# Attention scores as three fp32r products of high and low parts, in a fused transformer layer on one core

## The chip, the core and the metric

The kernel runs on one core of a Trainium2 chip. A core has five engines with a queue each: TensorE (PE, with its weight loads PEld), VectorE (DVE), ScalarE (ACT), GpSimd (POOL) and SyncE (SP), which here only issues DMA transfers. They work in their own written order and wait for one another by semaphores. The metric is the device time of one execution in microseconds.

## What is computed

128 independent batches of 32 queries with 256 features; each batch has a context of 257 rows of 192 features.

```python
x = x + xattn(layernorm(x), ctx)      # 8 heads of 64: softmax(q k^T / 8) v, then Wo and bo
x = x + attn(layernorm(x))            # gated recurrent attention over the 32 positions, 4 heads of 64
x = x + ffn(layernorm(x))             # gelu(x U1 V1 + b1) U2 V2 + b2, hidden size 1024

# in xattn, for each batch:
q = x @ Wq; k = context @ Wk; v = context @ Wv
attn = softmax(einsum('bhsd,bhld->bhsl', q, k) * scale)
out = einsum('bhsl,bhld->bhsd', attn, v) @ Wo + bo

# in attn, w, r = sigmoid(...), k, v projections of xn:
state = (1 - w_t) * state + k_t v_t^T ;  out_t = r_t state
```

## The kernel before

The batches are worked on in 16 groups of G = 8, so that a group has T = 256 tokens. The program is one long pipeline, unrolled by Python: for each i (a group) and b (0 to 7), with n = 8i+b, every engine does its share for batch n, and fills the rest with pieces of the token-wise work of neighbouring groups. This text calls such a piece of the program **step b0 to b7**. It begins on TensorE with the transposition of the probabilities of batch n.

In a step TensorE does `turn_probs(n)` (L400, four transpositions), `score(n + 1)` (L388 and L391), the fillers of `FILL1[b]`, `pv(n)` (L413 to L418), and the fillers of `FILL2[b]`. The keys are never formed: `Qk` is Wk times q, per head (tiles Qa0, Qa1, Qb, buffers `qk`), and a score is Qk times the transposed context `raw_t`. The 192 context features are a part of 128 rows (L388) and a part of 64 rows (L391), the two halves of the (query, head) rows using the two row halves of the array. All of this is in fp32. Other projections (`terms`, L331) are already written as three products of high and low parts in fp32r, a reduced format of 4 bytes: high times high, low times high, high times low.

The softmax of batch n+1 goes DVE `nmax` (L765), ACT `exps` (L624), DVE `rinv` and `probs` (L770, L772), and must be done before the next step's transposition. ACT does in each step `pt_out(n)` (L629), `exps(n + 1)`, its part of the fillers, `pc_out(n)` (L634). GpSimd waits for `probs`, takes the last context column (L962), and has a few steps of its own in `STEPS`: the decays times k and r (`hat`), residual additions, and the inverse roots of the variances.

Filler names: XT, XT2, XT3 are transpositions of the three normalised inputs; q0 to q3, z, k, r, v projections; Qa0, Qa1, Qb the three parts of Qk; Sp, Sq the products of rhat and khat (L510); O2, Y1, Y2, Y3 outputs of the three parts; Pf, H0 (with H1), H2 (with H3), Qf the feed-forward part, with H the hidden tiles whose gelu ACT computes (L691); TP and WV the value side; psp, su, i0 to i2, ti, pr, cf are VectorE's. Each filler writes one or two of four PSUM banks, taken in turn over the whole program; a bank is written again when the tile four before has been read out.

SyncE issues in each step `load_t(n + 3)` and `load_n(n + 3)` into rings of three buffers. `load_n` waits until PV of batch n has finished, and all that stands behind it waits too. In b5 the 16 small transfers of `load_tail_values` (L274) stand ahead of `load_t(n + 3)`.

## Time and profile before

| | us |
|---|---|
| median of 3 runs | 1013.85 |
| lowest, highest | 1013.67, 1015.03 |
| the profiled execution | 1017.14 |
| its span, first to last instruction | 1015.4 |
| TensorE busy | 984.8 (97%) |
| ACT, VectorE, GpSimd busy | 571.6, 497.0, 211.0 |
| one group of eight batches in the middle | 59.6 |

The profile gives for each engine its busy time, and for each group of instructions the idle time ahead of it with the instruction that ended it. The stretches of a group repeat to within some hundredths of a microsecond from group 3 to group 13, so one group is enough to read. Times inside the trace are microseconds from the span's start.

### The profile page before, as it was taken

Reading aid. Unit: us, or ns where it says so; the run is one execution under the profiler, and the core shown is the slowest. Engines: PE = TensorE matmul, PEld = TensorE weight load, DVE = VectorE, ACT = ScalarE, POOL = GpSimd, SP = SyncE. Lnnn points to the kernel's source line nnn. Section 1 sums busy time; section 2 is a strip of 40 time slices with the busy share of each in tenths; the row PEclk is TensorE's granted clock in tenths of the full one; section 3 lists DMA queues with packets and bytes.
Section 4 is the critical chain, followed back from the end, with each engine's and each line's share of the span. In section 5 each row is a group of like instructions: output and inputs, shape, how many; then the busy total and the mean of one; then the engine's idle time right before and its main releaser. Section 6 shows DMA issues by size and latency. Waiting matters only on the chain.

```text
span 1015.4 us, 21353 instructions
## 1 busy us (share of the span) xinstructions
PE 984.8 (97%) x8328; PEld 790.1 (78%) x8328; DVE 497.0 (49%) x1172; ACT 571.6 (56%) x1371; POOL 211.0 (21%) x356
## 2 busy tenths in 40 slices
PE   4999999999999999999999999999999999999997
PEld 3668787887878778787887878778787887877775
DVE  4444545463645546364554636454463545446252
ACT  3445457476574747657474765747466574746231
POOL 0010304022130302213031221303122040302130
PEclk9999999999999999999999999999999999999799
DMA  8232222222222221222222122222213222212000
GB/s 299 90 91 84 86 84 68 90 61 67 84 78 88 74 78 55 85 85 77 77 85 77 54 87 85 77 76 86 68 55 92 86 69 77 75 60 64 1 12 21
DMA packets 58002, 78.90 MB, mean 78 GB/s; under 512 B 10288, under 2 KB 39856, under 8 KB 57904
## 3 DMA queue, kind: packets, MB, share of 16 engines
q1 hardware_dynamic: 56192, 76.38, 24.3%
q8 instruction: 68, 1.11, 0.4%
q10 hardware_dynamic: 1712, 1.16, 0.4%
q14 instruction: 30, 0.25, 0.1%
HBM read 73.05 MB, written 4.46 MB: 76 GB/s over the span
## 4 chain that ended last, share of the span: by engine, by line
PE 69%; DVE 15%; ACT 12%; issue 2%; POOL 1%; DMA 0%; POOLq 0%; DVEq 0%
PE gb L331 13%; PE scores L388 9%; PE scores L391 6%; PE gb L450 6%; PE gb L510 5%; PE acc L417 5%; PE ptp L400 5%; PE acc L413 4%; DVE inv L865 4%; ACT probs L624 3%; PE acc L418 3%; PE gb L559 3%; DVE probs L772 2%; DVE nmax L765 2%; ACT hid L691 2%
## 5 line engine op out<-in xcount | busy, mean ns | idle before, releaser
L624 ACT ACTIVATE probs<-scores,nmax 128x257 f32<-128x257 f32 x256 | 119.4, 472 | 176.3 <-DVE nmax L765 176.1
L765 DVE TENSOR_REDUCE nmax<-scores 128x2 f32<-128x514 f32 x128 | 88.6, 692 | 215.8 <-PE scores L391 215.8
L962 POOL TENSOR_TENSOR ptm<-probs,head 128x32 f32<-128x32 f32 x128 | 33.1, 258 | 550.0 <-DVE probs L772 550.0
L388 PE MATMUL scores<-raw_t,qk 128*128 128x257 f32 x512 | 133.2, 383 | 1.3 <-ACT qk L664 1.3
L388 PEld LDWEIGHTS scores<-raw_t,qk 128*128 128x128 f32 x512 | 87.8, 191 | 8.8 <-issue 1.7
L772 DVE TENSOR_TENSOR probs<-probs,rinv 128x514 f32<-128x514 f32 x128 | 89.4, 699 | 4.4
L391 PE MATMUL scores<-raw_t,qk 64*128 64x257 f32 x512 | 90.7, 431 | 0.0
L417 PE MATMUL acc<-pt,raw_n 128*128 128x256 f32 x256 | 90.0, 433 | 0.0
L400 PE MATMUL ptp<-ident,probs 128*128 128x128 f32 x512 | 78.6, 276 | 9.2 <-DVE probs L772 7.5
L413 PEld LDWEIGHTS acc<-pt,raw_n 128*64 128x64 f32 x1024 | 55.8, 137 | 38.2 <-issue 24.5
L413 PE MATMUL acc<-pt,raw_n 128*64 128x128 f32 x1024 | 83.3, 284 | 0.6 <-ACT pt L629 0.4
L629 ACT ACTIVATE pt<-ptp 128x512 f32<-128x512 f32 x128 | 77.1, 602 | 11.8 <-PE ptp L400 9.9
L418 PE MATMUL acc<-pt,raw_n 128*128 128x256 f32 x256 | 76.6, 381 | 0.0
L770 DVE RECIPROCAL rinv<-rsum 128x2 f32<-128x2 f32 x128 | 21.0, 164 | 111.2 <-ACT probs L624 110.5
L634 ACT ACTIVATE pc<-acc 128x384 f32<-128x384 f32 x128 | 63.8, 498 | 20.2 <-PE acc L418 20.1
L1035 POOL TENSOR_TENSOR rstd<-ve,half 128x2 f32<-128x2 f32 x48 | 33.4, 696 | 200.4 <-DVE ve L753 200.3
L400 PEld LDWEIGHTS ptp<-ident,probs 128*128 128x128 f32 x512 | 60.3, 143 | 17.4 <-DVE probs L772 14.4
L391 PEld LDWEIGHTS scores<-raw_t,qk 64*128 64x128 f32 x512 | 38.7, 185 | 43.0 <-issue 43.0
L510 PEld LDWEIGHTS gb<-rhat,khat 64*128 64x128 f32 x1024 | 64.2, 193 | 3.2 <-issue 2.0
L510 PE MATMUL gb<-rhat,khat 64*128 64x32 f32 x1024 | 62.2, 273 | 1.3 <-POOL khat L1002 1.2
L331 PE MATMUL gb<-wo_h,o_h 128*128 128x256 f32 x192 | 57.1, 297 | 0.1
L417 PEld LDWEIGHTS acc<-pt,raw_n 128*128 128x128 f32 x256 | 38.3, 188 | 22.1 <-issue 22.1
(145 smaller groups left out, 2311.1 us busy)
## 6 DMA issues: line engine op xcount, KB each, us to landing
raw_t<-in_ctx_t SPq DMA_DIRECT2D x128, 258.0 KB, 2.9
raw_n<-in_ctx_n SPq DMA_DIRECT2D x128, 192.0 KB, 2.4
xb<-in_x SPq DMA_DIRECT2D x16, 256.0 KB, 2.7
vsp<-tail_values SPq DMA_DIRECT2D x256, 2.0 KB
out<-ob SPq DMA_DIRECT2D x16, 256.0 KB, 2.2
xin<-in_x SPq DMA_DIRECT2D x15, 256.0 KB, 2.9
khat<-in_wq ACTq DMA_DIRECT2D x1, 512.0 KB, 4.4
wv<-in_wv SPq DMA_DIRECT2D x1, 512.0 KB, 6.3
```

Of the source, the lines that this page charges most:

```text
L331: last = mm(out_, w, x, start=k == 0, stop=k == len(products) - 1)
L388: mm(scores[:, r, 0:L], w[:, b, r * P:(r + 1) * P], x[:, 0, 0:L], start=True, stop=False)
L391: mm(scores[:, r, 0:L], w[half, b, 2 * P:3 * P], x[half, 1, 0:L], start=False, stop=True).then_inc(s["scores_ready"], 1)
L400: last = nc.tensor.transpose(ptp[:, t, r * P:(r + 1) * P], probs[n % 2][:, r, t * P:(t + 1) * P], ident[:])
L413: last = mm(acc[64 * k:64 * k + 64, 1, 0:P], x[:, t, P:C], pt[:, t, k * P:(k + 1) * P], start=t == 0, stop=t == 1)
L417: mm(acc[:, 0], x[:, 0, 0:P], pt[:, 0], start=True, stop=False)
L418: mm(acc[:, 0], x[:, 1, 0:P], pt[:, 1], start=False, stop=True).then_inc(s["acc_ready"], 1)
L510: last = mm(out_[:, 0, t_].rearrange("p (b i) -> p b i", i=S)[:, :, block], khat[r0:r0 + 64, keys:keys + P], rhat[r0:r0 + 64, c * T + t * ...
L624: go(probs[n % 2][:, r, 0:L], scores[:, r, 0:L], ACT.Exp, bias=nmax[:, r:r + 1], accum_out=rsum[:, r:r + 1]).then_inc(s["exp_ready"], 1)
L629: go(pt[:], ptp[:], ACT.Copy).then_inc(s["ptev_ready"], 1)
L765: v_.tensor_reduce(nmax[:], scores[:, :, 0:L], AX.X, ALU.max, negate=True)\
L772: v_.tensor_tensor(p_[:, :, 0:L], p_[:, :, 0:L], rinv[:].rearrange("p (r o) -> p r o", o=1).to_broadcast([P, 2, L]), ALU.mult).then_inc(s[ ...
```

## The change

- **Scores.** `score` makes three fp32r products for each fp32 product: Qk high times context high, Qk low times context high, Qk high times context low. It reads 258 columns (LP) instead of 257.
- **Context parts.** `t_h` (the context rounded to fp32r) and `t_l` (what is left) have two buffers each. For batch m both are made in step m-2: the high part by ACT (`high`, between `pt_out` and `exps`), for two batches in eight by GpSimd; the low part by GpSimd (`parts`, ahead of all else in its step). TensorE waits for `low_ready`, and so does `load_t`, in place of the scores.
- **Qk parts.** ACT writes `qk_h`, VectorE subtracts for `qk_l` (items Qa0+1, Qa1+1, Qb+1 of `GAPS`).
- **Gelus.** H0 and H2 stand in the same step b7. Other fillers move: see the two tables `FILL1` and `FILL2`.
- **rhat** moves from GpSimd (r0, r1) to VectorE (`rh`), with the sigmoid's halving folded into Wo2, and the khat items move to b5.
- **Buffers.** Several tiles share memory (qs in hid, kt in ob, vt in at, qf in pr, xt3 in xt2, xn2 in xn1, xt1 in o), with waits for their last readers. The start-up constants go from before the first batch to step b3 of group 0; the third and later loads of `xin` go from b7 to b0 of the next step of i.

```diff
-FILL1 = [["Sq", "Qf", "WV"], ["O2"], [], ["Qa0"], [], ["Qa1", "H0"], ["Qb"], ["Sp", "H2"]]
-FILL2 = [[], ["Y3", "Y1", "XT"], ["q0", "q2", "Y2", "XT2"], ["z", "q1", "XT3"], ["q3", "r", "Pf"], ["k"], ["v"],
+FILL1 = [["Sq", "Qf", "WV"], ["O2"], [], ["Qa0"], ["Qa1"], ["Qb"], [], ["Sp", "H0", "H2"]]
+FILL2 = [[], ["Y3", "Y1", "XT"], ["Y2", "XT2", "q0", "q2"], ["z", "q1", "q3", "XT3"], ["k"], ["r"], ["Pf", "v"],
          ["TP"]]
...
+POOL_HIGH = (3, 4)
+def by_pool(m):
+    return (m - 2) % G in POOL_HIGH
...
             def load_t(n):
                 if n >= RING:
-                    sp.wait_ge(s["scores_ready"], 2 * (n - RING + 1))
+                    sp.wait_ge(s["low_ready"], n - RING + 1)
                 sp.dma_start(raw_t[n % RING][:], ctxt_v[n]).then_inc(ctxt_in[n % RING], 16)
...
             def score(n):
                 g, b = n // G, n % G
-                pe.wait_ge(ctxt_in[n % RING], 16 * (n // RING + 1))
+                pe.wait_ge(s["low_ready"], n + 1)
...
+                terms_ = ((w_h, h), (w_l, h), (w_h, l))
                 for r in range(2):
-                    mm(scores[:, r, 0:L], w[:, b, r * P:(r + 1) * P], x[:, 0, 0:L], start=True, stop=False)
-                for r in range(2):
-                    half = slice(64 * r, 64 * r + 64)
-                    mm(scores[:, r, 0:L], w[half, b, 2 * P:3 * P], x[half, 1, 0:L], start=False,
-                       stop=True).then_inc(s["scores_ready"], 1)
+                    for k, (w, x) in enumerate(terms_):
+                        mm(scores[:, r, 0:LP], w[:, b, r * P:(r + 1) * P], x[:, 0], start=k == 0, stop=False)
+                for k, (w, x) in enumerate(terms_):
+                    for r in range(2):
+                        half = slice(64 * r, 64 * r + 64)
+                        last = mm(scores[:, r, 0:LP], w[half, b, 2 * P:3 * P], x[half, 1], start=False, stop=k == 2)
+                        if k == 2:
+                            last.then_inc(s["scores_ready"], 1)
...
+            def high(m):
+                act.wait_ge(ctxt_in[m % RING], 16 * (m // RING + 1))
+                if m > 1:
+                    act.wait_ge(s["scores_ready"], 2 * (m - 1))
+                go(t_h[m % 2][:], raw_t[m % RING][:], ACT.Copy).then_inc(s["high_act_ready"], 1)
...
                     if 0 <= n < B:
                         pt_out(n)
+                    if (i, b) == (FIRST, 4):
+                        high(0)
+                    if 0 < n + 2 < B and not by_pool(n + 2):
+                        high(n + 2)
                     if 0 <= n + 1 < B:
                         exps(n + 1)
...
+            def parts(m):
+                if m > 1:
+                    pool.wait_ge(s["scores_ready"], 2 * (m - 1))
+                if by_pool(m):
+                    pool.wait_ge(ctxt_in[m % RING], 16 * (m // RING + 1))
+                    p_.tensor_copy(t_h[m % 2][:], raw_t[m % RING][:]).then_inc(s["high_pool_ready"], 1)
+                    pool.wait_ge(s["high_pool_ready"], m + 1 - act_highs(m))
+                else:
+                    pool.wait_ge(s["high_act_ready"], act_highs(m))
+                p_.tensor_tensor(t_l[m % 2][:], raw_t[m % RING][:], t_h[m % 2][:].bitcast(F32), ALU.subtract)\
+                    .then_inc(s["low_ready"], 1)
...
-                    [["Y2-2"], ["XT2-1", "xn2-2"], []],
-                    [[], ["su-1"], ["i0-1", "i1-1", "i2-1", "ti-1"]],
-                    [["r-1", "ln0+2"], ["pr-1", "cf-1"], []],
-                    [["xn0+2"], [], []],
-                    [[], [], ["S0-1", "S1-1"]]]
+                    [["Y2-2"], ["XT2-1", "xn2-2"], ["Qa0+1"]],
+                    [[], ["su-1"], ["Qa1+1", "ti-1", "i0-1"]],
+                    [[], ["cf-1"], ["Qb+1", "i1-1"]],
+                    [["i2-1", "pr-1"], [], ["rh-1", "ln0+2"]],
+                    [[], ["S0-1", "S1-1"], ["xn0+2"]]]
```

The order of instructions shows where the pieces stand. First ACT in steps b6 and b7, before. `pt` begins a step, `probs` are the exponentials, `qk` the copies of Qb, `hid` the gelus of H2.

```order
L629 ACTIVATE pt<-ptp 128x512
L624 ACT_TABLE_LOAD
L624 ACTIVATE probs,rsum<-scores,nmax 128x257 x2
L664 ACTIVATE qk<-gb 128x2x8x32 x2
L634 ACTIVATE pc<-acc 128x12x32
L682 ACTIVATE vt<-gb 128x512
L629 ACTIVATE pt<-ptp 128x512
L624 ACTIVATE probs,rsum<-scores,nmax 128x257 x2
L691 ACT_TABLE_LOAD
L691 ACTIVATE hid<-gb,vecs 128x256 x4
L634 ACTIVATE pc<-acc 128x12x32
```

The same two steps of the changed kernel; the lines are those of its own text, `t_h` is the high copy, the `at` row is the copy of v.

```order
L659 ACTIVATE pt<-ptp 128x512
L655 ACTIVATE t_h<-raw_t 128x516
L648 ACTIVATE probs,small<-scores,small 128x257 x2
L664 ACTIVATE pc<-acc 128x12x32
L720 ACTIVATE pf<-gb 128x256
L716 ACTIVATE at<-gb 128x512
L659 ACTIVATE pt<-ptp 128x512
L655 ACTIVATE t_h<-raw_t 128x516
L648 ACTIVATE probs,small<-scores,small 128x257 x2
L725 ACT_TABLE_LOAD
L725 ACTIVATE hid<-gb,vecs 128x256 x8
L664 ACTIVATE pc<-acc 128x12x32
```

In b6 and b7 a copy of raw_t for the batch after next now stands ahead of the exponentials, the copies of Qb are gone to b5, and all eight gelus stand in b7.

SyncE from b4 to b7 of the changed kernel, where the order is the same as before but for the load of `xin`, which stood ahead of the third raw_t load:

```order
L270 DMA raw_n<-in_ctx_n 128x384
L293 DMA vsp<-tail_values 8x64 x16
L265 DMA raw_t<-in_ctx_t 128x516
L270 DMA raw_n<-in_ctx_n 128x384
L265 DMA raw_t<-in_ctx_t 128x516
L270 DMA raw_n<-in_ctx_n 128x384
L265 DMA raw_t<-in_ctx_t 128x516
L270 DMA raw_n<-in_ctx_n 128x384
L275 DMA xin<-in_x 128x2x256
```

The first raw_t behind the vsp transfers is that of batch 8g+8, the first batch of the next group. Only what waits for it has moved.

## Rows read from the trace of the kernel before

**Rows 1.** The page: busy time, share of the span, instructions.

```profile
PE 984.8 (97%) x8328; PEld 790.1 (78%) x8328; DVE 497.0 (49%) x1172; ACT 571.6 (56%) x1371; POOL 211.0 (21%) x356
```

**Rows 2.** Stretches b0 to b7 of group 9: length, engines' busy time, clock, DMA.

```profile
535.15:545.97 10.82, 10.82 (x123) 7.87 (x122) 3.54 (x8) 4.96 (x11) 0.24 (x1) 1.00 0.15 44
545.97:554.56 8.59, 8.59 (x74) 7.49 (x73) 3.53 (x7) 3.04 (x8) 0.24 (x1) 1.00 0.38 110
554.56:561.42 6.86, 6.86 (x54) 5.87 (x53) 4.72 (x13) 3.04 (x9) 0.94 (x2) 1.00 0.44 144
561.42:568.43 7.01, 7.01 (x56) 5.93 (x55) 4.34 (x12) 5.42 (x14) 0.93 (x2) 1.00 0.19 57
568.43:574.95 6.52, 6.52 (x48) 5.38 (x47) 4.20 (x9) 4.20 (x11) 1.27 (x2) 1.00 0.15 43
574.95:581.69 6.74, 6.74 (x53) 5.53 (x52) 5.98 (x19) 4.11 (x9) 2.02 (x4) 1.00 0.03 6
581.69:588.10 6.41, 6.26 (x54) 4.48 (x52) 1.56 (x3) 6.37 (x16) 4.17 (x7) 1.00 0.43 131
588.10:594.76 6.66, 6.66 (x68) 5.58 (x69) 2.25 (x5) 5.02 (x12) 3.35 (x6) 1.00 0.30 94
sum 59.61, PE 59.46 PEld 48.13 DVE 30.11 ACT 36.15 POOL 13.18; mean PE 7.43 PEld 6.02 DVE 3.76 ACT 4.52 POOL 1.65
```

**Rows 3.** Timeline of ACT and VectorE in b1: start, duration, instruction, idle before.

```profile
548.88 0.48 ACT L624 ACTIVATE probs<-scores,nmax 128x257 f32<-128x257 f32 x1 [1.67 <-DVE nmax L765]
...
548.15 0.69 DVE L765 TENSOR_REDUCE nmax<-scores 128x2 f32<-128x514 f32 x1 [1.67 <-PE scores L391]
...
550.13 0.69 DVE L772 TENSOR_TENSOR probs<-probs,rinv 128x514 f32<-128x514 f32 x1
```

**Rows 4.** Timeline of TensorE in b1: the score, and two fp32r products.

```profile
546.40 1.03 PE L388 MATMUL scores<-raw_t,qk 128*128 128x257 f32 x4
547.37 0.70 PE L391 MATMUL scores<-raw_t,qk 64*128 64x257 f32 x4
...
551.53 0.28 PE L331 MATMUL gb<-wo_l,o_h 128*128 128x256 f32 x1
551.65 0.28 PE L331 MATMUL gb<-wo_h,o_h 128*128 128x256 f32 x1
```

**Rows 5.** Timeline of TensorE in b4 and b5: PV, half-row pairs, next step.

```profile
568.43 0.60 PE L400 MATMUL ptp<-ident,probs 128*128 128x128 f32 x4
...
570.47 0.66 PE L413 MATMUL acc<-pt,raw_n 128*64 128x128 f32 x8
...
576.89 0.38 PE L363 MATMUL gb<-qs,wk 64*128 64x256 f32 x1
...
577.76 0.38 PE L549 MATMUL gb<-pf,v 64*128 64x256 f32 x1
...
578.72 0.66 PE L413 MATMUL acc<-pt,raw_n 128*64 128x128 f32 x8
...
581.69 0.27 PE L400 MATMUL ptp<-ident,probs 128*128 128x128 f32 x1
```

**Rows 6.** Groups by line: busy time, mean ns, idle before.

```profile
L652 ACT ACTIVATE xt_h<-xt 128x512 fp32r<-128x512 f32 x16 | 10.1, 629 | 0.5
L691 ACT ACT_TABLE_LOAD x28 | 35.9, 1283 | 0.5
L1025 POOL TENSOR_TENSOR xb<-xb,bo 128x512 f32<-128x512 f32 x16 | 20.5, 1279 | 0.0
L818 DVE TENSOR_TENSOR o_l<-gb,o_h 128x512 fp32r<-128x512 f32 x32 | 20.7, 687 | 64.1 <-ACT o_h L666 64.0
```

**Rows 7.** Line L772 (minimum, median, maximum ns), and GpSimd's groups at L1002.

```profile
L772 DVE TENSOR_TENSOR probs<-probs,rinv x128: 694/695/1121, 24.6 to 940.1; 128x514 f32<-128x514 f32 x128
...
L1002 POOL TENSOR_TENSOR khat<-ke,cf 128x128 f32<-128x128 f32 x16 | 12.8, 800 | 2.9 <-DVE cf L878 0.7
L1002 POOL TENSOR_TENSOR khat<-ke,cf 128x256 f32<-128x256 f32 x16 | 10.4, 651 | 0.0
```

**Rows 8.** SyncE's timeline b4 to b6; landing of raw_t; waits of its reader.

```profile
572.59 9.36 SPq L274 DMA_DIRECT2D vsp<-tail_values  x16
582.00 0.44 SPq L246 DMA_DIRECT2D raw_t<-in_ctx_t  x1
...
DMA to landing us min/median/max: 2.6/2.9/9.6
...
  DMA raw_t<-in_ctx_t: 0.2, 1
```

**Rows 9.** Idle times of TensorE, and the granted clock (column after the busy times) behind them.

```profile
25.35 0.73 PE L400 MATMUL ptp<-ident,probs 128*128 128x128 f32 x4 [2.81 <-DVE probs L772]
...
25.80:29.20 3.40, 3.40 (x14) 1.91 (x14) 0.17 (x1) 0.60 (x1) 0.00 (x0) 0.50 0.00 0
...
942.63 0.64 PE L510 MATMUL gb<-rhat,khat 64*128 64x32 f32 x8 [1.16 <-POOL khat L1002]
...
954.20:957.60 3.40, 3.40 (x26) 1.73 (x28) 0.78 (x2) 0.00 (x0) 0.00 (x0) 0.50 0.00 0
...
984.69 0.65 PE L559 MATMUL gb<-hid,u 128*64 128x256 f32 x4 [1.28 <-ACT hid L691]
...
984.70:990.00 5.30, 5.13 (x74) 4.45 (x74) 0.77 (x2) 0.39 (x1) 3.20 (x4) 1.00 0.01 3
```

More of the change, by code:

```diff
@@ L102, with act_highs @@
 BANK = bank_table()
-HATS = 9
+HATS = 7
+POOL_HIGH = (3, 4)
+def by_pool(m):
+    return (m - 2) % G in POOL_HIGH
+def act_highs(m):
+    return sum(not by_pool(j) for j in range(m + 1))
 DECAYS = 5
@@ L158, in build @@
         pt = sb("pt", [P, LT, 256])
-        nmax, rsum, rinv = sb("nmax", [P, 2]), sb("rsum", [P, 2]), sb("rinv", [P, 2])
-        qk = [sb(f"qk{i}", [P, G, 256 + P]) for i in range(2)]
+        small = sb("small", [P, 8])
+        nmax, rsum, rinv, warm = (small[:, 2 * k:2 * k + 2] for k in range(4))
+        qk_h, qk_l = ([sb(f"{n}{i}", [P, G, 256 + P], F32R) for i in range(2)] for n in ("qk_h", "qk_l"))
+        t_h, t_l = ([sb(f"{n}{i}", [P, 2, LP], F32R) for i in range(2)] for n in ("t_h", "t_l"))
         pc = sb("pc", [P, H + H // 2, T])
@@ L190, in build @@
         s2 = sb("s2", [P, 8, P])
[L193 to L206 removed]
+        o2_h, o2_l, xt3, xn2 = xt2_h, xt2_l, xt2, xn1
+        pf = sb("pf", [P, T])
+        wxt_raw, ww_raw, vt_all = hid[:, 0:2], hid[:, 2:4], rhat[:]
+        tail_t = ke[:, 0:256].rearrange("p (c b) -> p c b", c=2)
+        mask_raw, bw_raw = ke[:, 256:256 + P], ke[:, 384:386]
+        wq_raw, kv2_raw = khat[:, 0:1024], khat[:, 1024:2048]
+        wr2_raw, wo2_raw = (x[:].rearrange("p c d -> p (c d)") for x in (at, xt2))
+        wo_raw = s2[:].rearrange("p t q -> p (t q)")
         scores = ps("scores", [P, 2, 512])
@@ L301, in _ @@
                         load_tail_values(i)
-                    if b == 7 and i + 3 < NG:
-                        load_x(i + 3)
+                    if b == 0 and 3 <= i + 2 < NG:
+                        load_x(i + 2)
                     if n + RING < B:
@@ L643, in step @@
                     if n == "XT":
[L644 removed]
+                        go(xt1_h, t[:], ACT.Copy).then_inc(s["xt1_h_ready"], 1)
                     elif n == "XT2":
```

115 lines of the change are left out of this document (65 added, 50 removed).

## Prediction

> **What bounds the kernel now.** I read the page's busy times first, then the stretches of one group of eight batches, then the matmuls in order of time, and last the queue of SyncE. TensorE is busy for 97% of the span [rows 1]. The group from 535.15 us is cut at the first transposition of each batch into eight stretches, which I call steps b0 to b7 (step b of group g transposes the probabilities of batch n = 8g+b, computes the scores of n+1, and fills in other work). They add to 59.61 us; TensorE is idle for 0.15 us of that, all in b6, where ACT is busy for 6.37 of 6.41 us [rows 2]. So matmul time is the bound nearly everywhere, and what TensorE saves counts in full as long as nothing new is late at the start of a step. What must be in time there is the softmax of n+1: score, maximum, exponentials, reciprocal, normalisation. From the exponentials' start (548.88) to the end of the normalisation (550.13 + 0.69) it takes 1.94 us, and from the maximum's start 2.67 [rows 3]. With 0.07 us after the scores and 0.05 before the next transposition a step can't be shorter than about 2.10 + 2.8 = 4.9 us before, and 4.7 after; all eight have room.
>
> **Scores.** An fp32 product is two instructions in the trace. Four for 128 rows go from 546.40 to 547.37, then those for 64 rows follow [rows 4]. Eight fp32 instructions of 64 rows and 256 columns, two at a time, fill 577.76 - 576.89 = 0.87 us: one holds the array 0.217 us [rows 5]; four fill 0.87 of the 0.97, and 0.10 go to the switch to 64 rows, which stays. An fp32r product of 256 columns is one instruction and follows the last after 0.118 us (551.53, 551.65) [rows 4]. Six of these for four fp32: 0.71 for 0.87, saves 0.16. The 64-row products run two at a time on different row halves: 0.217 us for a pair in fp32. For a pair in fp32r no row exists. Bounds: 0.118 if they run together like the fp32 ones, 0.236 if one after the other. I take 0.118, since the fp32 pairs, the nearest row, do run together [rows 5]. Three pairs for two: 0.35 for 0.43, saves 0.08. Together 0.24 us a batch; at the other bound it is a loss of 0.11. 128 batches: 30 us, if all of it shows.
>
> **What ACT and GpSimd get.** The high copy is an ACT copy of 128x516 from SBUF; the nearest is 128x512 with 0.629 us. The gelus go from two table switches a group to one: two loads of 1.28 us less (one to gelu, one back), against six copies of 0.63; so ACT gains 1.2 us a group on 36.15, no bound [rows 2, 6]. The low part on GpSimd is a subtraction of two SBUF tiles of 516 columns: 1.28 us by its 128x512 addition [rows 6]; the high copies of two batches a group lie between 0.6 and 1.28. Some 12.8 us more on its 13.2, of 60: it has room, and a low part begins some 1.9 us into its step and is needed 0.44 us into the next. VectorE gets six Qk subtractions of 0.69 [rows 6]; they stand behind the normalisation, push the next maximum by up to 0.7 us in b5 and b6, and are covered by 0.5 to 1 us of room there. The eight gelus run from about 5.3 to 8.2 us after b7's start and end 0.9 us into b0, the longest step: covered. Before the second pair of hidden tiles TensorE waits some 0.1 us for two banks. Shared buffers and their waits (qf in pr, kt in ob, vt in at, xt3 in xt2) have sources that are done a step earlier: nothing.
>
> The trace has one place where VectorE and GpSimd get in each other's way: the normalisation takes 0.695 as a rule and 1.121 once, and GpSimd's 128x128 product takes 0.80 where the 128x256 one takes 0.65 [rows 7]. The Trainium skill says why ("SBUF — State Buffer", section "Who interferes with whom"): a VectorE instruction with two SBUF inputs and a GpSimd instruction that reads SBUF exclude each other for their whole length. By that rule each of the 128 new subtractions could hold a normalisation up by 1.28 us; the order places them 1 to 2 us ahead of it, so the sum would be the same but for a tenth of a microsecond in b6.
>
> **The fillers** move only between steps. Y2 and XT2 stand ahead of q0 and q2; q3 goes from b4 to b3 (+0.71 there); b4 loses q3, r and Pf and gains Qa1 and k; b5 has Qb and r; b6 has Pf and v; b7 gains H0 (0.87). With -0.24 each: b0 10.58, b1 8.35, b2 6.62, b3 7.48, b7 7.38 (with the wait for banks). b4 has its PV at 2.04 - 0.24 + 0.87 = 2.67 us, then PV and k take 2.97 as in b5 of before (578.72 to 581.69): 5.64. In the same way b5 5.83 and b6 5.78: 17.25 us for b4 to b6. Unhindered, a group would take 57.7.
>
> **The wait that I expect.** Before, raw_t(m) is first read by TensorE in step m-1. Now ACT copies it in step m-2, ahead of the exponentials of m-1, and ACT works in order. For seven batches of eight the load lands early enough. For m = 8g+8 it doesn't: SyncE issues it behind raw_n(8g+7), which waits for PV of 8g+4 (b4), and behind the 16 small transfers of vsp, 9.36 us long. Before, it is issued at 582.00, 13.57 us after b4's start, with PV at 2.04 [rows 5, 8]. Now PV stands 0.63 later: 14.20. It lands 2.9 us later (2.6 the least) [rows 8], at 17.1. ACT would copy it 1.3 us into b6, that is at 12.8. It waits 4.3 us, and the exponentials of 8g+7 wait behind it. Then copy 0.65 with start, 1.94 to the end of the normalisation, 0.05: b7 starts at 14.20 + 2.9 + 0.05 + 0.65 + 1.94 + 0.05 = 19.8 instead of 17.25. TensorE has done all it may and stands idle for 2.5 us. The group is then 10.58 + 8.35 + 6.62 + 7.48 + 19.8 + 7.38 = 60.2, 0.6 more than before.
>
> The rest: groups 2 to 14 (13) 0.6 each, 8 us. Group 15 has no load behind its vsp transfers: -1.9. Group 1, with fewer fillers, about +1. Group 0: b4 to b6 again 19.8 in place of 15.9 and the other five steps -1.2: +2.7; constants now stand in VectorE's b3, but their delay (some 4 us) is swallowed by this same wait. The Qk low part ahead of the first score: one subtraction, +0.7. The last 64 us: no term that I can see. Sum: 8 - 1.9 + 1 + 2.7 + 0.7 = +10.5 us on the profiled run's 1017.14, or, by the same difference, 1013.85 + 10.5 = 1024 in the median.
>
> **The clock.** In this trace the granted clock fell from 2.4 to 1.2 GHz after an idle time of 2.81 us (at 25.8, for 3.4 us) and after 1.16 us followed by the narrow products of rhat and khat (from 944 on, and still at 957.6, though TensorE was busy throughout), and stayed at 2.4 GHz after 1.28 us [rows 9]. An idle time of 2.5 us is nearer to the first, and b7 begins with a transposition and a score and then has these narrow products. 3.4 us at half clock lose 1.7, 13.6 us some 6; I take 3.5 a fall. Whether all 15 waits bring one can't be read from three cases: I take half, 26 us; the ends are 0 and 15 x 4 = 60.
>
> **Rivals.**
> - *The forecast*: wait and falls in part of the groups: 1024 + 26 = about 1049 us; with 5 to 15 falls 1035 to 1084. Chance 0.62.
> - *Wait without falls*, as after the idle 1.28 us: 1024, between 1016 (landing 2.6, a smaller start) and 1034. Chance 0.22.
> - *The load comes in time* (the other side). The wait decides nothing if raw_t(8g+8) lands by 17.25 - 2.69 = 14.56 us after b4's start, 2.5 us earlier than computed: if the vsp transfers took under 7 us or PV of b4 ended earlier. For it: before, TensorE waits for such a load once, for 0.2 us [rows 8]. Against it: 9.36 us is the issue time of SyncE itself, the same in every group, and 2.6 the least landing. Then each of 16 groups saves 1.9, the start costs some 1.5: 1013.85 - 29 = 985. Chance 0.08.
> - *Half-row pairs don't run together*: +0.35 a batch in the five steps outside b4 to b6, 28 us on top of the first or second case: 1050 to 1080. Chance 0.05, and the remaining 0.03 for anything later still, a second late softmax among it.
>
> **Numbers.** Predicted 1049 us. The range goes from 1016 (no falls, landing at its least) to 1085 (a fall in each group) and leaves out the full gain and a little above. A difference of 0.2% (2 us) is what a measurement can tell from no change: faster 0.09, within it 0.03 (the wait costing just what the scores save), slower 0.88.
>
> **What would show it.** ACT's copy t_h in b6 idle about 4 us before it with the transfer of raw_t named, once a group and in no other step; TensorE idle some 2.5 us before the transposition of 8g+7; b4 to b6 19.8 us together; score 1.26 us from its first to the next product instead of 1.50; two table loads a group; half clock in stretches after that idle time. I am wrong if the copy in b6 waits for nothing, if the clock row stays at full, or if a 64-row pair takes 0.24 us.

## The result, and the profile after

The changed kernel takes 1059.8 us in the median of 4 runs (1055.1 to 1068.8), where the kernel before took 1014.4 beside it (1013.7 to 1016.9): 1.046 times as long, 95% interval 1.042 to 1.050. The forecast was 1049 with a range of 1016 to 1085. The runs of the changed kernel differ by 13.7 us among themselves, those of before by 3.2. The profiled execution is the longest of the four, 1068.8 us with a span of 1066.6.

First the page of the changed kernel: busy time of the engines as in [rows 1], then the granted clock in 40 slices, and two groups of new instructions (the ACT copy t_h and GpSimd's t_l).

```profile
PE 989.1 (93%) x8840; PEld 832.3 (78%) x8840; DVE 613.2 (57%) x1285; ACT 581.3 (54%) x1439; POOL 367.8 (34%) x484
...
PEclk9889889999999999999998999999899999999998
...
L1032 POOL TENSOR_TENSOR t_l<-raw_t,t_h 128x516 fp32r<-128x516 f32 x128 | 164.6, 1286 | 263.8 <-PE scores L413 161.5
...
L655 ACT ACTIVATE t_h<-raw_t 128x516 fp32r<-128x516 f32 x96 | 61.3, 639 | 67.0 <-DMA raw_t<-in_ctx_t 67.0
```

TensorE went from 97% to 93% of the span: it now waits, and some of its busy time is at half clock. The last row names the wait: ACT's copy of the context stood 67.0 us idle for the load of raw_t. In the table of waits (total us, times, longest) it is 15 waits, one a group:

```profile
ACT t_h L655 <- DMA raw_t<-in_ctx_t: 67.0, 15, 5.7
```

Then one group, group 6, cut at the transpositions into b0 to b7 as in [rows 2] (length, busy time of PE, PEld, DVE, ACT, POOL, clock, DMA share, GB/s):

```profile
380.92:391.91 10.99, 10.82 (x126) 7.94 (x126) 3.68 (x8) 5.73 (x13) 1.53 (x2) 1.00 0.22 67
391.91:400.25 8.34, 8.34 (x77) 7.69 (x76) 3.28 (x7) 3.56 (x9) 1.52 (x2) 1.00 0.35 113
400.25:407.19 6.94, 6.84 (x58) 6.08 (x56) 5.43 (x13) 3.61 (x10) 1.95 (x2) 1.00 0.44 142
407.19:414.79 7.60, 7.59 (x64) 6.80 (x65) 5.93 (x14) 6.01 (x16) 4.88 (x7) 1.00 0.19 63
414.79:420.45 5.66, 5.66 (x50) 4.87 (x49) 3.58 (x9) 3.73 (x11) 0.64 (x2) 1.00 0.05 6
420.45:426.26 5.81, 5.81 (x58) 4.75 (x57) 5.52 (x11) 4.01 (x10) 3.79 (x5) 1.00 0.12 36
426.26:434.41 8.15, 5.79 (x46) 4.94 (x44) 5.36 (x9) 3.75 (x10) 4.61 (x7) 1.00 0.45 147
434.41:441.94 7.53, 7.52 (x80) 6.40 (x81) 4.61 (x14) 5.91 (x15) 3.99 (x5) 1.00 0.01 2
sum 61.02, PE 58.38 PEld 49.47 DVE 37.40 ACT 36.31 POOL 22.91; mean PE 7.30 PEld 6.18 DVE 4.68 ACT 4.54 POOL 2.86
```

TensorE does 58.4 us of work where it did 59.5, and the group is 61.0 long instead of 59.6. The idle time stands in b6 (2.36 us), with 0.17 in b0 and 0.10 in b2. The chain through b6, from the timelines of SyncE, ACT, VectorE and TensorE (start, duration, instruction, idle before and what ended it):

```profile
419.58 9.36 SPq L293 DMA_DIRECT2D vsp<-tail_values  x16
428.98 0.44 SPq L265 DMA_DIRECT2D raw_t<-in_ctx_t  x1
```

```profile
431.74 0.63 ACT L655 ACTIVATE t_h<-raw_t 128x516 fp32r<-128x516 f32 x1 [4.19 <-DMA raw_t<-in_ctx_t]
432.29 0.46 ACT L648 ACTIVATE probs<-scores,small 128x257 f32<-128x257 f32 x1
...
433.52 0.84 DVE L811 TENSOR_TENSOR probs<-probs,small 128x514 f32<-128x514 f32 x1
...
434.42 0.66 PE L423 MATMUL ptp<-ident,probs 128*128 128x128 f32 x4 [2.36 <-DVE probs L811]
```

The load is issued 14.19 us after b4's start (forecast 14.20), the copy begins at 16.95 (17.15), b7 at 19.63 (19.8).

In groups 1 to 14 TensorE's idle time in front of b7 lies between 2.31 and 4.60 us, and what varies is the load: SyncE takes 9.36 us over the 16 transfers in nine of these groups and up to 10.64 in the others (in group 8 one of the sixteen takes 1.60 us instead of 0.54), and raw_t lands 2.68 to 3.02 us after its issue, in group 11 after 4.29.

Last the clock. Group 8 had a wait in b6 like every other (3.36 us, one of the longer ones), and what followed ran at 1.2 GHz (column after the busy times: 0.50):

```profile
559.08 0.66 PE L423 MATMUL ptp<-ident,probs 128*128 128x128 f32 x4 [3.36 <-DVE probs L811]
```

```profile
560.20:570.40 10.20, 10.20 (x68) 8.24 (x67) 3.48 (x11) 6.13 (x15) 3.62 (x4) 0.50 0.01 2
```

That b7 took 12.11 us instead of 7.53. In this execution the clock fell behind 7 of the 15 waits, for 3.4 to 13.7 us. Idle times of 2.31 to 2.53 us were followed by no fall in seven groups and by one in the eighth; 3.06 us by none; the other six, 2.64 to 4.60 us, by one each.

### The profile page after: what moved, and what is told of

Its sections match the earlier page's. It is cut to its first block, busy times and chain, and to the rows that moved or that the text cites. A ratio compares the mean times of both kernels' runs of the same rounds, so it can differ in the third digit from the quotient of the medians.

```text
span 1066.6 us, 23095 instructions
## 1 busy us (share of the span) xinstructions
PE 989.1 (93%) x8840; PEld 832.3 (78%) x8840; DVE 613.2 (57%) x1285; ACT 581.3 (54%) x1439; POOL 367.8 (34%) x484
## 4 chain that ended last, share of the span: by engine, by line
PE 61%; SPq 13%; DVE 8%; ACT 6%; issue 6%; DMA 5%; POOL 2%; DVEq 0%; POOLq 0%; ACTq 0%
SPq L293 13%; PE gb L350 9%; PE scores L409 6%; PE gb L473 6%; PE gb L534 5%; PE acc L440 5%; PE scores L413 5%; PE ptp L423 4%; PE acc L436 4%; DMA raw_t<-in_ctx_t 4%; PE acc L441 3%; ACT probs L648 3%; PE gb L573 3%; PE gb L583 3%; DVE xn L798 3%
## 5 line engine op out<-in xcount | busy, mean ns | idle before, releaser
L1032 POOL TENSOR_TENSOR t_l<-raw_t,t_h 128x516 fp32r<-128x516 f32 x128 | 164.6, 1286 | 263.8 <-PE scores L413 161.5
L648 ACT ACTIVATE probs<-scores,small 128x257 f32<-128x257 f32 x256 | 119.1, 471 | 143.2 <-DVE small L804 143.0
L804 DVE TENSOR_REDUCE small<-scores 128x2 f32<-128x514 f32 x128 | 88.2, 689 | 122.5 <-PE scores L413 122.4
L655 ACT ACTIVATE t_h<-raw_t 128x516 fp32r<-128x516 f32 x96 | 61.3, 639 | 67.0 <-DMA raw_t<-in_ctx_t 67.0
L811 DVE TENSOR_TENSOR probs<-probs,small 128x514 f32<-128x514 f32 x128 | 90.9, 710 | 4.4
L409 PE MATMUL scores<-t_h,qk_h 128*128 128x258 f32 x256 | 85.6, 335 | 2.2 <-DVE qk_l L858 2.2
L809 DVE RECIPROCAL small<-small 128x2 f32<-128x2 f32 x128 | 20.7, 162 | 112.4 <-ACT probs L648 112.4
L436 PEld LDWEIGHTS acc<-pt,raw_n 128*64 128x64 f32 x1024 | 57.2, 140 | 30.2 <-issue 22.3
L409 PE MATMUL scores<-t_h,qk_l 128*128 128x258 f32 x256 | 74.6, 291 | 0.0
L409 PE MATMUL scores<-t_l,qk_h 128*128 128x258 f32 x256 | 74.4, 291 | 0.0
L858 DVE TENSOR_TENSOR qk_l<-gb,qk_h 128x512 fp32r<-128x512 f32 x96 | 61.6, 683 | 8.2 <-ACT qk_h L695 8.2
```

The source lines that it names most:

```text
L409: mm(scores[:, r, 0:LP], w[:, b, r * P:(r + 1) * P], x[:, 0], start=k == 0, stop=False)
L436: last = mm(acc[64 * k:64 * k + 64, 1, 0:P], x[:, t, P:C], pt[:, t, k * P:(k + 1) * P], start=t == 0, stop=t == 1)
L648: go(probs[n % 2][:, r, 0:L], scores[:, r, 0:L], ACT.Exp, bias=nmax[:, r:r + 1], accum_out=rsum[:, r:r + 1]).then_inc(s["exp_ready"], 1)
L804: v_.tensor_reduce(nmax[:], scores[:, :, 0:L], AX.X, ALU.max, negate=True)\
L811: v_.tensor_tensor(p_[:, :, 0:L], p_[:, :, 0:L], rinv[:].rearrange("p (r o) -> p r o", o=1).to_broadcast([P, 2, L]), ALU.mult).then_inc(s[ ...
L1032: p_.tensor_tensor(t_l[m % 2][:], raw_t[m % RING][:], t_h[m % 2][:].bitcast(F32), ALU.subtract)\
```

## The experiments

Each kernel was measured beside the kernel before on the same chip; a difference between two changed kernels is that of their medians and can cross chips, where the kernel before gave 1014.1 to 1015.5 us. "The group" is the middle of groups 3 to 13.

### The late load taken away

> The changed kernel with the 16 vsp transfers moved on SyncE from b5 to b7, between the loads raw_t and raw_n of that step; all else as in the changed kernel. Theory (raw_t of 8g+8 stands behind the vsp transfers and ACT's copy in b6 waits for it): ACT no longer waits for that transfer, b6 falls from 8.3 to about 5.8 us, TensorE's idle time of 2.5 us before the first transposition of b7 is gone, the clock falls behind it are gone too; 15 x 2.6 = 39 us and some 16 to 20 us of half clock: 1060 - 57 = about 1003 us (998 to 1010). Rival (it is the copies and subtractions themselves, on ACT and GpSimd, that make the softmax late): less than 10 us change, 1050 or more.

```diff
-                    if b == 5 and i < NG:
-                        load_tail_values(i)
...
                     if n + RING < B:
                         load_t(n + RING)
+                    if b == 7 and i < NG:
+                        load_tail_values(i)
+                    if n + RING < B:
                         load_n(n + RING)
```

Measured: 1018.0 us (1017.7 to 1019.3), 1.0043 (1.0027 to 1.006). The wait of t_h is gone from the table, b4 to b6 takes 17.84 us instead of 19.8, the clock stays at full from 84 to 988 us. So the load behind the 16 transfers is the cause of most of the loss. But 1018 is not the 1003 that was expected: the group is 59.23, not 57.7, and step b0 of group 1 takes 11.71 us where the kernel with the transfers in b6 (below) has 7.19. There WV of group 0 (L474) waits for the values that now land too late:

```profile
  DMA vsp<-tail_values: 2.9, 1
```

> Control: the kernel before with the same move of the vsp transfers from b5 to b7. Theory: nothing there reads raw_t before the step that needs it, so 1014 +- 2 us. Rival (the place of the vsp transfers costs by itself, by the DMA engines or SyncE's order): a change of more than 2 us, and part of what the move brings in the changed kernel would be no part of this explanation.

The same edit, made on the kernel before. Measured: 1020.3 (1020.0 to 1021.6), 1.0066 (1.005 to 1.0083): a miss, by 6 us. The middle groups are unchanged (59.5 to 59.6); b0 of group 1 went from 7.41 to 13.12, and b0 of group 2 from 9.09 to 9.88, with a wait of 0.71 us for the same transfers. It is the place of the transfers in b7 that costs, in groups 1 and 2 alone.

### The same, with the transfers in b6

The edit is the one above with `b == 6`.

> The changed kernel with one edit: the 16 transfers of vsp are issued in b6, between raw_t and raw_n, instead of in b5; nothing else. Theory: with them in b7 (measured 1018.02 us) the steady group was 59.23 us and group 1 alone paid some 4.5 us, because WV of group 0 waited for transfers that landed late. In b6 they stand one step earlier, so that this 4.5 us goes and nothing else changes: 1018.0 - 4.5 = 1013.5 us (1011 to 1016), steady group 59.2, b4 to b6 17.8 us, b0 of group 1 about 8 us in place of 11.71, no fall of the clock behind b6. Rival: the transfers stand in front of loads in b6 as they did in b5, and b4 to b6 is 19.8 us again in some groups with a fall of the clock behind it: above 1030 us. The kernel with four moves (992.92) minus this one is then what the three moves on ACT and VectorE are worth: 20.6 us by theory, 1.2 us in each of 13 groups and some 5 us in the others.

> The kernel before with the same edit: the transfers of vsp in b6, between raw_t and raw_n. With them in b7 it was 1020.31 us, 6 above the kernel before, all of it in groups 1 and 2. If that was the late landing in front of WV of group 0, one step earlier takes it away: 1014.4 (1012 to 1017), steady group 59.6 as in the kernel before, since there no engine waited for the load behind them. If the move itself costs something on any queue, it stays at 1018 or above; if the load behind the transfers did cost something in the kernel before, it falls under 1012.

Measured: the changed kernel with it 1013.7 us (1011.5 to 1017.1, 12 runs), 0.9989 (0.9976 to 1.0002); the kernel before with it 1015.8 (1013.1 to 1017.3), 1.0007 (0.9994 to 1.0019). Both as the theory had it. In the kernel before the place of the transfers is worth nothing; in the changed kernel it is worth 46 us (47, if each is held against the kernel before beside it). The change without its late load is no faster and no slower than the kernel before. Here are b6 and the group's sum of the first of the two, and TensorE's first instruction of b7:

```profile
581.98:588.35 6.37, 5.79 (x47) 4.94 (x45) 5.21 (x9) 3.61 (x10) 4.75 (x7) 1.00 0.24 73
...
sum 59.29, PE 58.40 PEld 49.52 DVE 37.25 ACT 36.27 POOL 23.07; mean PE 7.30 PEld 6.19 DVE 4.66 ACT 4.53 POOL 2.88
```

```profile
588.35 0.66 PE L424 MATMUL ptp<-ident,probs 128*128 128x128 f32 x4 [0.58 <-DVE probs L812]
```

An idle time of 0.58 us is left in b6, for the normalisation, and no load is late.

### The idle time filled, for the clock alone

> The changed kernel with five more fp32 products (ident x v1, 256 columns, into the ptp bank that is free then) at the end of TensorE's b6, in groups 0 to 14: they fill about 2.2 us of the idle time and compute nothing that is used. Theory (the rest of the loss is the half clock that follows the idle time): b4 to b6 stay at 19.7 us, no fall of the clock behind b6, b7 7.5 us in every group: 1060 - 16 (the excess of b7 over 7.5 us, summed over the groups) - a few = about 1040 us (1036 to 1045), and the spread between executions shrinks. Rival (the clock costs nothing that the late load doesn't cost anyway): 1055 to 1062.

```diff
                     for name, g in behind:
                         steps[name](g)
+                    if b == 6 and 0 <= i < NG - 1:
+                        for k in range(5):
+                            mm(ptp[:, 0], ident[:], v1[:, 0:256], start=True, stop=True)
```

Measured: 1043.1 us (1041.9 to 1044.2), 1.0292 (1.0272 to 1.0312). The wait is there as before (b6 and b7 of group 8 and, below, the stretch of nearly all groups, clock in the third column from the right):

```profile
540.04:548.13 8.09, 7.96 (x56) 6.69 (x54) 5.33 (x9) 3.74 (x10) 4.57 (x7) 1.00 0.46 141
548.13:555.66 7.53, 7.52 (x80) 6.39 (x81) 4.61 (x14) 5.92 (x15) 4.00 (x5) 1.00 0.03 12
```

```profile
64.80:1040.00 975.20, 950.84 (x8684) 801.78 (x8682) 576.57 (x1218) 550.99 (x1369) 350.66 (x461) 1.00 0.23 71
```

b7 is 7.52 us in every group from 2 on. So the clock's share of the loss is 1059.8 - 1043.1 = 16.7 us, and it is also the scatter: the runs now lie within 2.2 us instead of 13.7. The wait itself is the rest of the 46: 1043.1 - 1013.7 = 29.4 us.

### The copy behind the exponentials, in b6 only

> The changed kernel with ACT's high copy behind the exponentials in b6 alone. Theory (the exponentials of 8g+7 are late because they stand behind the copy): the softmax of 8g+7 is in time, b6 is 5.8 us; now the score of 8g+8 in b7 waits for the low part: landing 17.1 + copy 0.7 + subtraction 1.3 = 19.1 us after b4's start, where the score is due at 17.25 + 0.44 = 17.7: idle 1.4 us in b7 in place of 2.5 before it. 15 x 1.1 = 16 us less and fewer falls of the clock: about 1033 us (1024 to 1045). Rival (the exponentials are late for the transfer's other effects): no change, 1055 or more.

```diff
-                    if 0 < n + 2 < B and not by_pool(n + 2):
+                    if 0 < n + 2 < B and not by_pool(n + 2) and b != 6:
                         high(n + 2)
                     if 0 <= n + 1 < B:
                         exps(n + 1)
+                    if 0 < n + 2 < B and b == 6:
+                        high(n + 2)
```

Measured: 1054.7 (1050.8 to 1056.2), 1.0397 (1.0371 to 1.0424), far over what was expected. The order of ACT was indeed what held b7 up: b4 to b6 is 17.84. But the score in b7 now waits for the low part, as expected:

```profile
483.43 0.66 PE L423 MATMUL ptp<-ident,probs 128*128 128x128 f32 x4 [0.57 <-DVE probs L813]
485.75 0.39 PE L409 MATMUL scores<-t_h,qk_h 128*128 128x258 f32 x1 [1.67 <-POOL t_l L1034]
```

Two idle times, 0.57 and 1.67 us, with a transposition between them, and this b7 took 14.02 us, part of it at half clock. The clock fell behind b6 in 5 of the 15 groups; where it held, b7 took 8.6 in the middle, 1.1 more than with no wait. The first half of the theory stands (who blocks whom); the second half, that shorter idle times leave the clock alone, fell.

### Two of the sixteen transfers behind the load

> The changed kernel with 14 of the 16 vsp transfers in b5 as there, and two moved to b7 between raw_t and raw_n. Theory (b7 starts at the issue of raw_t of 8g+8 plus 5.5 us): raw_t is issued 2 x 0.586 = 1.2 us earlier, b4 to b6 19.7 - 1.2 = 18.5 us, TensorE idle 1.2 to 1.4 us behind b6 in groups 2 to 14. Without clock falls 1043 (the kernel with a filled idle time) - 15 x 1.2 = 1025 us; whether an idle time of 1.3 us brings falls is what this run tells: none, 1023 to 1027; some, up to 1040. Rival (the late load is a matter of the DMA engines' backlog, not of the queue's order): b4 to b6 stay above 19.

```diff
                     if b == 5 and i < NG:
-                        load_tail_values(i)
+                        load_tail_values(i, range(7))
...
                     if n + RING < B:
                         load_t(n + RING)
+                    if b == 7 and i < NG:
+                        load_tail_values(i, range(7, 8))
```

Measured: 1039.4 (1036.2 to 1049.8), 1.0265 (1.0207 to 1.0323). `load_tail_values` gets the heads as an argument; 14 transfers stay ahead of the load and 2 go behind it. The load is earlier by the 1.17 us of two transfers, and b4 to b6 is 18.44 to 18.55 us in seven groups, as expected: the wait scales with SyncE's queue, by the time of the transfers that were moved. Here a b7 with no fall of the clock, and one with:

```profile
619.02 0.66 PE L426 MATMUL ptp<-ident,probs 128*128 128x128 f32 x4 [1.20 <-DVE probs L814]
```

```profile
619.02:626.55 7.53, 7.53 (x80) 6.41 (x81) 4.61 (x14) 5.89 (x14) 3.99 (x5) 1.00 0.02 6
```

```profile
494.84 0.33 PE L426 MATMUL ptp<-ident,probs 128*128 128x128 f32 x1 [2.70 <-DVE probs L814]
```

```profile
494.84:506.93 12.09, 12.09 (x81) 10.15 (x81) 4.61 (x14) 6.75 (x17) 3.99 (x5) 0.58 0.00 1
```

In this profile idle times of 1.17 to 1.27 us in b6 were followed by no fall, seven times in seven, and 1.56 us by none; the other seven, 1.89 to 4.26 us, were followed by one each. Within this profile the clock goes with the length of the idle time, but 2.31 to 2.53 us brought a fall only once in eight in the changed kernel above. The idle time differs from group to group by the load again: in the seven short cases raw_t is issued 13.02 to 13.10 us after b4's start and lands in 2.72 to 2.79 us; in the others it is issued at 13.23 to 13.73, or lands only after 3.60 to 4.71, or both.

### The two copies ahead of the normalisation, in b0

> The changed kernel with the vsp transfers in b7 (as in e1_vsp_later) and with VectorE's copies of S2 and S3 in b0 ahead of the normalisation instead of behind it. Theory (in b0 the exponentials are late by the table load behind the eight gelus, the copies of S2 and S3 behind the normalisation with them, and the WV products wait for S2's bank): b0 10.98 falls to about 10.65 us; 13 x 0.33 = 4 us less than 1018, 1014 (1012.5 to 1015.5). Rival (the 0.4 us in b0 are the products' own time): 1018 and b0 10.98.

```diff
-            GAPS = [[["psp-1"], [], ["S2-2", "S3-2", "WV0-1", "WV1-1"]],
+            GAPS = [[["psp-1"], ["S2-2", "S3-2"], ["WV0-1", "WV1-1"]],
```

Added to the first experiment's kernel. Measured: 1014.9 (1011.9 to 1017.2, 10 runs), 1.0001 (0.9984 to 1.0018), against 1018.0 without; b0 is 10.59 instead of 10.98. What held WV up was a bank that VectorE read out behind a normalisation. Why the normalisation is late is read from ACT's timeline in b0, and no run tests it. In the changed kernel, group 6 (b0 from 380.92):

```profile
382.18 0.70 ACT L655 ACTIVATE t_h<-raw_t 128x516 fp32r<-128x516 f32 x1
382.89 1.28 ACT L648 ACT_TABLE_LOAD   x1
384.19 0.48 ACT L648 ACTIVATE probs<-scores,small 128x257 f32<-128x257 f32 x1
```

The eight gelus are over 0.56 us into b0, and `pt` starts only 0.11 us later than before (0.78 instead of 0.67). The table load starts 0.68 us later (1.97 instead of 1.29), most of it for the high copy that now stands ahead of it, and the exponentials start at 3.27 instead of 2.94.

### Four moves together

> The changed kernel with the vsp transfers in b6 between raw_t and raw_n, S2 and S3 copies ahead of the normalisation in b0, VectorE's maximum ahead of xn1 in b2 and ahead of i2 and pr in b6. Theory (with the late load gone, what is left is VectorE being late in b2 and b6, and S2's bank in b0): b0 10.65, b2 6.65, b6 5.85 us, no idle time of TensorE over 0.2 us from group 2 to 14; a group of 58.1 in place of 59.2: 14 x 1.1 = 15 us, and 4 us in group 1, whose b0 waited for the vsp transfers: 1018 - 19 = about 999 us (995 to 1004), faster than the kernel before. Rival (the late maximum in b6 comes from TensorE or ACT): b6 stays at 6.36 and the time above 1008.

```diff
-                    if b == 5 and i < NG:
-                        load_tail_values(i)
...
+                    if b == 6 and i < NG:
+                        load_tail_values(i)
...
-            GAPS = [[["psp-1"], [], ["S2-2", "S3-2", "WV0-1", "WV1-1"]],
+            GAPS = [[["psp-1"], ["S2-2", "S3-2"], ["WV0-1", "WV1-1"]],
...
-                    [["XT+1", "xn1-1"], [], []],
+                    [["XT+1"], ["xn1-1"], []],
...
-                    [["i2-1", "pr-1"], [], ["rh-1", "ln0+2"]],
+                    [[], ["i2-1", "pr-1"], ["rh-1", "ln0+2"]],
```

Measured: **992.9 us** (992.0 to 994.6), 0.9779 (0.9761 to 0.9797), under the expected 995 to 1004 and 2.2% faster than the kernel before. Against the kernel with only the transfers moved it is 20.8 us less; so three moves of VectorE's items, none of which removes an instruction, are worth nearly as much as the faster scores (23.9 us, below). The page, b2, b6 and the sum of group 9:

```profile
PE 955.5 (97%) x8840; PEld 809.0 (82%) x8840; DVE 611.8 (62%) x1285; ACT 584.8 (59%) x1439; POOL 368.1 (37%) x484
```

```profile
546.92:553.60 6.68, 6.68 (x58) 6.13 (x57) 6.47 (x17) 4.22 (x11) 3.37 (x5) 1.00 0.50 150
...
572.61:578.46 5.85, 5.79 (x46) 4.93 (x44) 5.63 (x9) 3.42 (x10) 4.57 (x7) 1.00 0.23 75
...
sum 58.00, PE 57.94 PEld 49.44 DVE 37.33 ACT 36.63 POOL 22.85; mean PE 7.24 PEld 6.18 DVE 4.67 ACT 4.58 POOL 2.86
```

TensorE's idle time is down to 0.06 us a group.

### The score's share

> e10_four_moves with the scores as one fp32 product again (Qk high times context high, read as fp32; the low parts are still made and not used). Theory (the three fp32r products save 0.24 us a batch where nothing else is late): 128 x 0.23 = 29 us slower than e10_four_moves. Rival (half-row pairs in fp32r or the reads of the low parts cost it again): less than 15 us slower.

```diff
-                terms_ = ((w_h, h), (w_l, h), (w_h, l))
+                h, w_h = h.bitcast(F32), w_h.bitcast(F32)
+                terms_ = ((w_h, h),)
...
-                        last = mm(scores[:, r, 0:LP], w[half, b, 2 * P:3 * P], x[half, 1], start=False, stop=k == 2)
-                        if k == 2:
+                        last = mm(scores[:, r, 0:LP], w[half, b, 2 * P:3 * P], x[half, 1], start=False, stop=True)
+                        if k == 0:
```

The kernel is that of the four moves. Measured: 1016.8 us (1015.7 to 1019.7, 10 runs), 23.9 more than with the three products, where 29 were expected. That is 0.19 us a batch. In b3 the step went from 7.53 to 7.76, in b6 only from 5.83 to 5.89, in part because VectorE holds its end up in the faster kernel (b6 is 5.72 there in the groups where TensorE doesn't wait for it). The score of b3 in the changed kernel, with fp32r, and the same place in the kernel of this experiment, with fp32 (TensorE's timelines):

```profile
407.61 0.37 PE L409 MATMUL scores<-t_h,qk_h 128*128 128x258 f32 x1
407.82 0.28 PE L409 MATMUL scores<-t_h,qk_l 128*128 128x258 f32 x1
407.94 0.28 PE L409 MATMUL scores<-t_l,qk_h 128*128 128x258 f32 x1
...
408.51 0.39 PE L413 MATMUL scores<-t_h,qk_h 64*128 64x258 f32 x2
...
408.97 0.37 PE L382 MATMUL gb<-hid,wk 64*128 64x256 f32 x1
```

```profile
568.41 1.04 PE L411 MATMUL scores<-t_h,qk_h 128*128 128x258 f32 x4
569.38 0.71 PE L415 MATMUL scores<-t_h,qk_h 64*128 64x258 f32 x4
569.91 0.38 PE L383 MATMUL gb<-hid,wk 64*128 64x256 f32 x1
```

From its first product to the next filler the score takes 1.36 us instead of 1.50 (forecast 1.26). Six fp32r products for 128 rows take 0.90 us to the first of the 64-row ones, not 0.81 (six at 0.118 and 0.10 for the switch): the first of them holds the array for 0.21. Four fp32 instructions take 0.97. The score is thus 0.14 us shorter, and there is a second part: from the start of the step to the first product of the score it is 0.35 to 0.41 us instead of 0.43 to 0.47. The two together make up most of the 0.18 to 0.25 us by which every step but b6 differs.

### GpSimd's subtraction taken away

> The changed kernel with the vsp transfers in b7 (as in e1_vsp_later) and GpSimd's subtraction of the low part replaced by a memset of t_l to zero, which reads nothing from SBUF and is shorter (the low part of the context is left out). Theory (VectorE and GpSimd exclude each other, and that makes VectorE late in b2 and b6): in b2 the second xn takes 0.4 instead of 1.3 us, in b5 the first cf copy 0.2 instead of 0.73; the cf steps beside the khat items stay long; b2 6.6 us, b6 6.0 us: 13 x 0.7 = 9 us less than 1018, about 1009 (1006 to 1012). Rival (the VectorE work of Qk itself makes it late): durations and time as in e1_vsp_later.

```diff
-                p_.tensor_tensor(t_l[m % 2][:], raw_t[m % RING][:], t_h[m % 2][:].bitcast(F32), ALU.subtract)\
-                    .then_inc(s["low_ready"], 1)
+                p_.memset(t_l[m % 2][:].bitcast(F32), 0.0).then_inc(s["low_ready"], 1)
```

Measured: 1003.3 us (1002.1 to 1004.7), 14.7 less than the first experiment's kernel, where 9 were expected. b2 went from 6.94 to 6.64 to 6.68 and b6 from 6.36 to between 5.85 and 6.03. VectorE's and GpSimd's timelines in b2, first of the changed kernel, then without the subtraction:

```profile
402.94 1.62 DVE L798 TENSOR_SCALAR xn<-x,mv,rstd 128x256 f32<-128x256 f32 x2 [0.28 <-POOL rstd L1105]
404.48 0.68 DVE L804 TENSOR_REDUCE small<-scores 128x2 f32<-128x514 f32 x1
...
402.80 1.28 POOL L1032 TENSOR_TENSOR t_l<-raw_t,t_h 128x516 fp32r<-128x516 f32 x1
```

```profile
558.99 0.83 DVE L799 TENSOR_SCALAR xn<-x,mv,rstd 128x256 f32<-128x256 f32 x2 [0.28 <-POOL rstd L1105]
559.74 0.68 DVE L805 TENSOR_REDUCE small<-scores 128x2 f32<-128x514 f32 x1
...
558.83 0.53 POOL L1033 MEMSET t_l<- 128x516 f32 x1
```

The same two VectorE instructions take 1.62 us beside the subtraction (the first of them 1.29) and 0.83 beside the memset, and the maximum behind them starts that much later. The two steps give 8.6 us in the groups 3 to 14 (0.72 each); groups 1, 2 and 15 give 3 more (2.98 by their lengths), and the last 3 are the clock: the first experiment's profile has 6.8 us at half clock from 988.7 on, this one has none there. By the two steps alone the expected 9 was right.

### The loops over the row halves exchanged

> e10_four_moves with the two loops of the 64-row products exchanged, so that the three products of one row half stand together and then the three of the other. Theory (pairs on different row halves run together only when they stand side by side): three more products of 0.12 us one after the other, less one that may overlap at the border: 0.24 to 0.36 us a batch, 30 to 45 us slower than e10_four_moves, a score slower than in fp32. Rival (the array takes them from anywhere in its queue): the same time as e10_four_moves.

```diff
-                for k, (w, x) in enumerate(terms_):
-                    for r in range(2):
+                for r in range(2):
+                    for k, (w, x) in enumerate(terms_):
```

Measured: 993.9 us (993.5 to 994.7), 0.9801 (0.9774 to 0.9829), against 992.9 without the edit: the same, a plain miss. The timeline still has the 64-row products in twos:

```profile
530.43 0.39 PE L414 MATMUL scores<-t_h,qk_h 64*128 64x258 f32 x2
530.65 0.29 PE L414 MATMUL scores<-t_h,qk_l 64*128 64x258 f32 x2
530.77 0.29 PE L414 MATMUL scores<-t_l,qk_h 64*128 64x258 f32 x2
530.89 0.87 PE L535 MATMUL gb<-rhat,khat 64*128 64x32 f32 x14
```

The program now issues three for one half and then three for the other, and they ran side by side all the same. The edit did not make the case it was to price, so this kernel gives no upper price for halves that don't overlap.

## Why the prediction was right, and where not

**The mechanism was right, and so was the length of the wait.** Each link was found: load issue 14.19 (14.20), ACT's wait 4.16 to 5.75 us in groups 1 to 14, 4.4 in the middle (4.3), and 2.38 in group 0, in no other step; TensorE's idle time 2.36 in group 6 (2.5), b4 to b6 19.6 to 19.8 us (19.8) in eight groups. In the others it is longer by the load, as above: the prediction took the 9.36 us of the 16 transfers as "the same in every group", but the trace of before has 9.36 or 9.37 us only in eight of sixteen groups and up to 10.07 in the others. The two experiments that move the transfers, and the one that moves two of sixteen, show that the length of that queue is the cause.

**The clock** was given 26 us and is worth 16.7. The count, half of the 15 waits, was good for the profiled execution (7 falls). Where a fall stretched b7, it added 1.4, 1.5, 1.5, 1.9, 4.6, 4.6 and 4.7 us, a mean of 2.9 with 0.9 more in one following b0: 3.0 a fall, where 3.5 was taken. That is 21 us in the longest of four executions, and a fall at 1038.1 us, behind the last group, cost it some 2.9 more (by 70.8 us for that stretch against 67.9 in the kernel with filled idle time); the median has less. Two numbers of that part don't follow from its own terms: 1024 + 26 is 1050, and 5 falls of 3.5 us give 1042, not 1035.

**The loss without the clock** was put at 10.5 us; it is 1043.1 - 1014.4 = 28.7. Cut by groups, the profile of the kernel with filled idle time lies above that of before by 2.9 us ahead of the first transposition (forecast 0.7), 3.6 in group 0 (2.7), 2.9 in group 1 (1) and 22.3 in groups 2 to 14 (8); group 15 is 0.2 shorter up to its last step (1.9), and what follows takes 67.9 us instead of 74.5, where the profile of before has 13.7 us at half clock. The forecast group was 60.2, the measured one 61.2 at full clock. The steps, in the middle of groups 3 to 13:

| | b0 | b1 | b2 | b3 | b4 | b5 | b6 | b7 | b4 to b6 |
|---|---|---|---|---|---|---|---|---|---|
| before | 10.82 | 8.59 | 6.87 | 7.01 | 6.52 | 6.73 | 6.41 | 6.66 | 19.66 |
| forecast | 10.58 | 8.35 | 6.62 | 7.48 | 5.64 | 5.83 | | 7.38 | 19.8 |
| after | 10.99 | 8.34 | 6.94 | 7.60 | 5.66 | 5.81 | 8.32 | 7.53 | 19.8 |
| transfers in b6 | 10.98 | 8.34 | 6.94 | 7.59 | 5.66 | 5.82 | 6.37 | 7.53 | 17.85 |
| four moves | 10.60 | 8.40 | 6.68 | 7.53 | 5.66 | 5.81 | 5.83 | 7.52 | 17.30 |

Three terms failed there:

- *"The eight gelus … end 0.9 us into b0, the longest step: covered."* They end earlier than that, at 0.56 us, and b0 is longer all the same. The exponentials start 3.27 us into b0, behind the high copy and the table load; the normalisation follows, VectorE's copies S2 and S3 stand behind it, and WV needs a bank that they read out: 0.4 us a group. The step named the room of the step and not the next reader in VectorE's queue, and it left the new high copy out of b0's chain.
- *"The sum would be the same but for a tenth of a microsecond in b6"*, on VectorE and GpSimd. The one normalisation of 1.121 us in [rows 7] was the warning. The prediction checked the normalisation against the new subtraction, and not VectorE's other instructions that stand ahead of a maximum: the first xn in b2 takes 1.29 us instead of 0.41, and in b6 the product pr takes 1.11 us instead of 0.42, beside GpSimd's khat products. The Trainium skill ("SBUF — State Buffer", section "Who interferes with whom") counts `tensor_scalar`, the form of xn, among the VectorE instructions that can take the ports shared with GpSimd, under conditions that no run here tests; the trace agrees, by 1.62 against 0.83 us for the same pair. The room in the steps was taken as unused where VectorE's busy time had gone from 1.56 us in b6 [rows 2] to 5.36. This costs 0.3 us a group in b2; the 0.6 in b6 are hidden behind the wait for the load and show only once that is gone.
- *The start.* One subtraction of 0.7 was counted ahead of the first score. There are three pairs of Qk low parts, each behind its ACT copy, and TensorE waits 2.18 us for the last of them (23.84 us). The first transposition comes at 28.83 us instead of 25.35; in the profiles of the changed kernel's variants it comes at 27.6 to 28.5, in those of before at 25.5 to 25.6. In group 0 b4 takes 8.0 us instead of 6.0 in every variant, since VectorE's constants stand ahead of a maximum there. The wait in b6 does swallow this, as forecast (b4 to b6 is 20.3 us, forecast 19.8); with the transfers in b6 it stays (17.5 instead of 15.9).

The last 64 us, where no term was seen, had none but the clock: with the transfers in b6 the stretch behind the last transposition takes 71.3 us in the kernel before and 67.9 in the changed one, and the profile of the first has 3.4 us at half clock twice there, that of the second none.

**The scores** save 0.19 us a batch over the whole kernel and up to 0.25 in steps that TensorE bounds, where 0.24 was forecast for all. The score itself is 0.14 shorter, not 0.24; the rest is won ahead of it, where no term was seen. The choice between the two bounds was right: the 64-row pairs run together (0.12 us to the next in the trace).

**The rival that was priced wrong** is "the load comes in time". It was given 985 us, all 1.9 us a group as gain. Made on the chip it is 1013.7: the group falls by 0.35 (59.6 to 59.25), and the other 1.55 are b0 (0.4), b2 (0.3), b3 (0.1), b6 (0.6) and b7 (0.15). It takes the three moves as well to come near it, 992.9. The rival "wait without falls", 1024 with a range to 1034, is the kernel with filled idle time: 1043.1, outside its range for the same terms.

So the total of 45.3 us is: 29.4 for the wait, 16.7 for the clock, and -0.7 for all else, in which some 24 us of faster scores are eaten by late work of VectorE and by the start. The forecast of 1049 came nearer than its terms deserved: the clock was 9 too high, the rest 18 too low, and that the two errors have opposite signs is luck. The 24 us are measured in the kernel with the four moves; how much of them shows in the changed kernel itself no run tells.
